# Making the ternary weights of the second feed-forward inside the channel mix of the layer ahead of it

## The chip, the cores and the metric

One core of a Trainium2 chip runs the whole program. The metric is the device time in microseconds (us) of one execution, median of several. Of the engines, TensorE (PE in the profile, its weight loads PEld), VectorE (DVE), ScalarE (ACT) and GpSimd (POOL) compute; SyncE (SP) issues most DMAs.

## The reference, cut to what matters

Two layers are computed for x of shape (16, 512, 16, 12): batch, nodes, channels, times. In each layer a conv part (attention over channels, attention over times, an attention over nodes combined with a graph convolution, a temporal convolution, a layer norm) is followed by a feed-forward: in layer 0 a mixture of eight experts, in layer 1 a two-matrix network whose weights are ternary. The change concerns the preparation of those ternary weights:

```python
def _weight_quant(w):
    s = jnp.clip(jnp.mean(jnp.abs(w)), EPS, None)
    w_dq = jnp.clip(jnp.round(w / s), -1.0, 1.0) * s
    return w + jax.lax.stop_gradient(w_dq - w)

# w_up is 1024 x 512, w_down 512 x 1024; EPS = 1e-05
h = _bitlinear(hidden_states, w_up, bits)      # activations rounded to 8 bits, weights ternary
h = jnp.square(jax.nn.relu(h))
out = _bitlinear(h, w_down, bits)
```

Each matrix needs one scalar, the mean of its absolute values, before any of its elements can be rounded.

## The kernel before, in words

The program is a row of stages. Each stage is one block: every engine has its own instruction list in it, the engines talk over semaphores, and all of them meet at the end of a block before the next begins. The stages of the second layer, in order, are `combine` (makes the layer's input from the experts' results), `conv_weights`, `small_attention` "c1" (16 x 16 attention over channels for all 16 items at once), `mix_channels` "m1" (applies it), `small_attention` "t1" (over times), `graph_conv` "g1", `quantise_weights` and `feed_forward`.

`mix_channels` (L524) goes over the 16 items of the batch. For each, SyncE loads the item's normalised rows (384 KB, four buffers), VectorE builds a 96 x 192 x 2 block matrix from the attention (L550, two buffers `k0`, `k1`; it waits until TensorE is done with item b-2), TensorE multiplies (L567, eight products, which the trace records as two each, as all f32 products) and ScalarE copies the sum to the large buffer `shared` (L579). GpSimd has no work in it. The loops are hardware loops of four items a turn.

`graph_conv` is the long stage. Its SyncE list begins with the load of item 0's rows, then calls `prefetch`, which in the second layer is `ternary_loads` (L1655): both raw weight matrices, 2 MB each, go into `shared`, which is free from then on. `quantise_weights` (L1668) comes after it, alone in its block, with 4096 elements to a partition for each matrix: VectorE sums the absolute values (L1684, one instruction for each matrix); TensorE adds up over the partitions by a product with ones (L1700); VectorE makes the scale and its inverse (L1686, L1687) and three passes over each matrix (L1689 multiply and add the rounding constant, L1690 subtract it and take the minimum with 1, L1691 the maximum with -1, written as bf16 to `wup` or `wdn`), then four small instructions (L1692 to L1695). `Chain` (its call is written `step(...)`) makes VectorE wait for the instruction just issued before it goes on.

`small_attention` "c1" has one more duty, in its SyncE list: `clear_retired` sets the semaphores of earlier stages to zero, one instruction each.

Of the kernel before, what the change touches and what calls it, by code (L numbers as in the profile page):

```python
# [16 lines left out]
F32 = mybir.dt.float32  # L17
# [44 lines left out]
def ready(n):  # L62

    return n + 1 + LEAD

def free(n, depth):

    return n + 1 + LEAD - depth

def dma_ready(i):

    return (i + 2) * 16
# [7 lines left out]
class Chain:  # L82

    def __init__(self, eng, sem):
        self.eng, self.sem, self.base, self.k = eng, sem, 0, 0

    def begin(self, base):
        self.base, self.k = base, 0
# [326 lines left out]
                        act.wait_ge(kept[q], dma_ready(B // 2 - 1))  # L416

def small_attention(nc, s, tag, chan, clear=False):

# [11 lines left out]
    with ExitStack() as ctx:  # L432
# [91 lines left out]
def mix_channels(nc, s, tag, xn_rows):  # L524

    with ExitStack() as ctx:
        (xn_in, big_done, mixed, out_done) = s.sems(
            tag,
            "xn_in*4 big_done mixed out_done")
        xnT, big = [s.xnT0, s.xnT1, s.raw0, s.raw1], [s.k0, s.k1]  # L530
        psm = [ctx.enter_context(nc.psum_tensor(f"{tag}_ps{q}", [P, 2, 512], F32)) for q in range(2)]
        with nc.Block() as block:
            @block.sync
            def _(sp):
                for z in range(4):
                    sp.sem_inc(xn_in[z], 16)
                with sp.Fori(0, B // 4) as i:
                    for z in range(4):
                        sp.wait_ge(mixed, free(i * 4 + z, 4))
                        sp.dma_start(xnT[z][0:HALF, :, :], xn_rows[i * 4 + z]).then_inc(xn_in[z], 16)  # L540

            @block.vector
            def _(dve):
                dve.sem_inc(big_done, LEAD)
                with dve.Fori(0, B // 4) as i:
                    for z in range(4):
                        b = i * 4 + z
                        dve.wait_ge(mixed, free(b, 2))
                        for h in range(2):
                            last = nc.vector.tensor_tensor(  # L550
                                big[z % 2][0:HALF, h, :].rearrange("p (c t) -> p c t", t=T),
                                s.rct[0:HALF, bass.ds(b * C, C)].unsqueeze(2).to_broadcast([HALF, C, T]),
                                s.tmask[:, h, 1, :].unsqueeze(1).to_broadcast([HALF, C, T]), ALU.mult)
                        last.then_inc(big_done, 1)

            @block.tensor
            def _(pe):
                pe.sem_inc(mixed, LEAD)
                with pe.Fori(0, B // 4) as i:
                    for z in range(4):  # L560
                        b = i * 4 + z
                        pe.wait_ge(xn_in[z], dma_ready(i))
                        pe.wait_ge(big_done, ready(b))
                        pe.wait_ge(out_done, free(b, 2))
                        for k in range(NK):
                            for h in range(2):
                                last = nc.tensor.matmul(psm[z % 2][:, k // 2, CT * (k % 2):CT * (k % 2) + CT],  # L567
                                                        xnT[z][0:HALF, h, P * k:P * k + P], big[z % 2][0:HALF, h, :],
                                                        start=(h == 0), stop=(h == 1))
                        last.then_inc(mixed, 1)  # L570

            @block.scalar
            def _(act):
                act.sem_inc(out_done, LEAD)
                with act.Fori(0, B // 4) as i:
                    for z in range(4):
                        b = i * 4 + z
                        act.wait_ge(mixed, ready(b))
                        nc.scalar.activation(  # L579
                            s.shared[:, bass.ds(b * (NK * CT), NK * CT)].rearrange("p (a x) -> p a x", a=2),  # L580
                            psm[z % 2][:, :, 0:2 * CT], ACT.Copy).then_inc(out_done, 1)
# [1070 lines left out]
                item_turns(act, turn)  # L1652

def ternary_loads(eng, s, d, loaded):  # L1655

    up, down = raw_ternary(s)
    eng.dma_start(up.rearrange("p (k i) -> p k i", k=NK),
                  d["w_up"].rearrange("(k p) i -> p k i", p=P)).then_inc(loaded, 16)
    eng.dma_start(down.rearrange("p (k n) -> p k n", k=UK),  # L1660
                  d["w_down"].rearrange("(k p) n -> p k n", p=P)).then_inc(loaded, 16)

def raw_ternary(s):
    return s.shared[:, 0:NK * UP], s.shared[:, NK * UP:2 * NK * UP]

def quantise_weights(nc, s, loaded):  # L1668

    W = NK * UP  # L1670
    with ExitStack() as ctx:
        (chain_done, summed) = s.sems("qw", "chain_done summed")
        w = raw_ternary(s)
        t = s.shared[:, 2 * W:3 * W]
        part = ctx.enter_context(nc.sbuf_tensor("qw_part", [P, 2], F32))
        inv = ctx.enter_context(nc.sbuf_tensor("qw_inv", [P, 2], F32))
        ps = ctx.enter_context(nc.psum_tensor("qw_ps", [P, 512], F32))
        with nc.Block() as block:
            @block.vector
            def _(dve):  # L1680
                step = Chain(dve, chain_done)
                for j in range(2):
                    dve.wait_ge(loaded, 32)
                    step(nc.vector.tensor_reduce(part[:, j:j + 1], w[j], AX, ALU.add, apply_absolute_value=True))  # L1684
                dve.wait_ge(summed, 1)
                step(nc.vector.tensor_scalar(s.wscale[:, :], ps[:, 0:2], 1.0 / (P * W), 1e-5, ALU.mult, ALU.max))  # L1686
                step(nc.vector.reciprocal(inv[:, :], s.wscale[:, :]))  # L1687
                for j, dst in enumerate((s.wup, s.wdn)):
                    step(nc.vector.tensor_scalar(t, w[j], inv[:, j:j + 1], MAGIC, ALU.mult, ALU.add))  # L1689
                    step(nc.vector.tensor_scalar(t, t, MAGIC, 1.0, ALU.subtract, ALU.min))  # L1690
                    step(nc.vector.tensor_scalar(dst, t, -1.0, None, ALU.max))  # L1691
                step(nc.vector.tensor_scalar(s.wscale[:, :], s.wscale[:, :], 1.0 / QB, None, ALU.mult))  # L1692
                step(nc.vector.tensor_copy(s.identb[:, :], s.ident[:, :]))
                nc.vector.memset(s.magic[:, :], MAGIC)
                nc.vector.memset(s.minus_magic[:, :], -MAGIC)  # L1695

            @block.tensor
            def _(pe):
                pe.wait_ge(chain_done, 2)
                nc.tensor.matmul(ps[:, 0:2], s.ones[:, :], part[:, :], start=True, stop=True).then_inc(summed, 1)  # L1700

def feed_forward(nc, s, x_in, x_out):
# [496 lines left out]
def build(nc, d, out):  # L2200
# [11 lines left out]
    def sb(ctx, name, shape, dt=F32):  # L2212
        return ctx.enter_context(nc.sbuf_tensor("s_" + name, shape, dt))

    with ExitStack() as top:
# [36 lines left out]
        with ExitStack() as ctx:  # L2252
            s.wscale, s.magic, s.minus_magic = (sb(ctx, n, [P, 2]) for n in ("wscale", "magic", "minus_magic"))
            s.identb = sb(ctx, "identb", [P, P], BF16)
            s.wup, s.wdn = (sb(ctx, n, [P, NK * UP], BF16)[:, :] for n in ("wup", "wdn"))
            with ExitStack() as conv:
                conv_buffers(nc, s, conv, 1)
                (loaded,) = s.sems("loads1", "loaded")
                combine(nc, s, "join", rows(raw_rows), 1e-6, rows(xn_rows), by_partition(x2),
                        prefetch=lambda eng: conv_loads(eng, s, d, 1, loaded))  # L2260
                conv_weights(nc, s, 1, loaded)
                s.sems.retire()
                small_attention(nc, s, "c1", True, clear=True)
                s.sems.reuse()
                (ternary,) = s.sems("loads2", "ternary")
                mix_channels(nc, s, "m1", rows(xn_rows))
# [63 lines left out]
```

## Time and profile before

| | |
|---|---|
| Median of three executions | 1864.14 us (1862.98 to 1868.24) |
| Profiled execution | 1862.88 us |
| Its span, first to last instruction | 1861.1 us |
| PE, DVE, ACT, POOL busy | 77%, 60%, 40%, 34% |
| c1, from its first product | 1189.5 to 1204.0 us |
| m1 | 1204.7 to 1253.4 us |
| t1, from its first product | 1253.7 to 1264.4 us |
| g1 | 1265.4 to about 1578.8 us |
| quantise_weights | 1579.1 to 1603.8 us |
| feed_forward | 1604.4 us to the end |

All times of the trace are counted from the first instruction of the profiled execution. [...] "128x512 f32" is 128 partitions of 512 elements each.

### The profile page before, as it was taken

The numbers are of one execution on the slowest core, as the hardware profiler recorded it, in microseconds if no ns is written. First come the engines' busy times: TensorE is split into PE (matmuls) and PEld (weight loads), VectorE is DVE, ScalarE is ACT, GpSimd is POOL, SyncE is SP. The second block draws the span as 40 slices with busy tenths as digits, with TensorE's granted clock in tenths as the row PEclk, the third lists the DMA queues.
The fourth block names the chain that finished last, engine by engine and source line by source line (L and its number), as shares of the span: only waits on it lengthen the run. The fifth ranks groups of instructions, "written<-read, shape, count | busy, mean of one in ns | idle before, by whom it ended". The sixth has DMA issues, their size and how long they took to land. (4 is left out here: it accounts for less than half of the span.)

```text
span 1861.1 us, 28248 instructions
## 1 busy us (share of the span) xinstructions
PE 1435.1 (77%) x8462; PEld 1179.6 (63%) x8462; DVE 1113.9 (60%) x2381; ACT 751.4 (40%) x1181; POOL 635.8 (34%) x918
## 2 busy tenths in 40 slices
PE   4578899999464289999999945497999994277676
PEld 4467788887343278888888834395888883155554
DVE  4622488888465654444445335313788886688886
ACT  2412455555242033333333224222555552177775
POOL 1100065556310446555555421000455565011111
PEclk7778899999697579999999965697999997588988
DMA  6423012221374046556555377343122121112221
GB/s 200 144 82 88 9 60 76 68 68 60 113 229 150 12 121 124 108 97 130 122 120 110 38 200 221 99 113 124 44 76 68 59 76 51 43 51 83 94 76 60
DMA packets 95966, 179.95 MB, mean 97 GB/s; under 512 B 13937, under 2 KB 31905, under 8 KB 95909
## 3 DMA queue, kind: packets, MB, share of 16 engines
q1 hardware_dynamic: 71828, 135.52, 23.1%
q0 software_dynamic: 16384, 31.51, 9.8%
q10 hardware_dynamic: 7696, 12.22, 2.1%
q8 instruction: 29, 0.48, 0.1%
q14 instruction: 29, 0.23, 0.0%
HBM read 113.12 MB, written 66.10 MB: 96 GB/s over the span
## 5 line engine op out<-in xcount | busy, mean ns | idle before, releaser
L731 PE MATMUL g_y<-L_z,L_pt 128*128 128x192 f32 x1024 | 197.5, 337 | 1.5 <-ACT L_pt L944 0.5
L889 POOL TENSOR_TENSOR L_xr<-L_xr,L_lnb 128x192 f32<-128x192 f32 x128 | 106.3, 859 | 208.1 <-DMA L_xr<-x 112.2
L731 PEld LDWEIGHTS g_y<-L_z,L_pt 128*128 128x128 f32 x1024 | 167.4, 194 | 6.8 <-ACT L_pt L944 6.8
L1269 POOL DMA_INDIRECT sums<-x_yo,x_places x64 | 103.0, 1609 | 136.4 <-ACT x_yo L1472 126.3
L936 ACT ACTIVATE L_e<-g_s,L_nm 128x512 f32<-128x512 f32 x128 | 88.0, 687 | 79.2 <-DVE L_nm L777 78.2
L699 PE MATMUL g_z<-L_kw,L_xnT 96*128 96x192 f32 x512 | 97.0, 344 | 26.1 <-DVE L_v L807 26.1
L699 PEld LDWEIGHTS g_z<-L_kw,L_xnT 96*128 96x128 f32 x512 | 87.1, 198 | 38.2 <-DVE L_v L807 38.2
L1381 DVE TENSOR_TENSOR x_mid<-ex_g,x_sig 128x480 f32<-128x480 f32 (+1 forms) x48 | 31.3, 653 | 132.8 <-ACT x_sig L1463 125.5
L896 POOL TENSOR_TENSOR L_t<-L_rstd 128x48 f32<-128x48 f32 x96 | 29.2, 305 | 224.5 <-DVE L_rstd L831 219.5
L777 DVE TENSOR_REDUCE L_nm<-g_s 128x1 f32<-128x512 f32 x128 | 87.5, 684 | 27.6 <-PE g_s L708 26.8
L786 DVE SCALAR_TENSOR_TENSOR L_p<-L_e,L_rl,L_adj 128x512 f32<-128x512 f32 x128 | 99.2, 775 | 4.7 <-DVE L_rl L784 0.3
L944 ACT ACTIVATE L_pt<-g_t 128x512 f32<-128x512 f32 x128 | 75.9, 593 | 48.1 <-PE g_t L716 47.9
L716 PE MATMUL g_t<-s_ident,L_p 128*128 128x128 f32 x512 | 77.6, 274 | 9.7 <-DVE L_p L786 9.7
L906 POOL TENSOR_TENSOR L_d<-L_d,L_lng 128x192 f32<-128x192 f32 x128 | 72.4, 598 | 35.7 <-DVE L_d L837 35.7
L1811 PE MATMUL ff_u<-s_wup,ff_q1s 128*96 128x512 bf16 x256 | 79.7, 468 | 5.4 <-DVE ff_q1s L1896 4.0
L716 PEld LDWEIGHTS g_t<-s_ident,L_p 128*128 128x128 f32 x512 | 63.2, 141 | 30.6 <-DVE L_p L786 25.5
L1254 POOL DMA_INDIRECT x_xin<-xn_rows,x_index x64 | 64.8, 1012 | 51.2 <-DVE x_index L1351 18.6
L1441 ACT ACTIVATE x_xh<-ex_t 128x480 fp32r<-128x480 f32 x64 | 36.5, 570 | 109.3 <-PE ex_t L1297 92.2
L727 PEld LDWEIGHTS g_y<-L_res,L_xnT 97*128 97x128 f32 x512 | 76.4, 196 | 6.4 <-ACT L_y L950 1.1
L1311 PE MATMUL ex_g<-x_xh,x_guh 128*128 128x480 f32 (+1 forms) x192 | 76.6, 399 | 3.1 <-issue 3.1
L1325 PE MATMUL ex_d<-x_wdh,x_hh 128*120 128x512 f32 (+1 forms) x192 | 77.5, 404 | 0.0
L1981 POOL TENSOR_TENSOR ff_yo<-ff_ya,ff_xr 128x768 f32<-128x768 f32 x16 | 29.6, 1852 | 139.0 <-DVE ff_ya L1935 139.0
(281 smaller groups left out, 3843.8 us busy)
## 6 DMA issues: line engine op xcount, KB each, us to landing
xn_rows<-L_xnT SPq DMA_DIRECT2D x48, 384.0 KB, 3.5
L_xnT<-xn_rows SPq DMA_DIRECT2D x48, 384.0 KB, 3.4
x<-L_y SPq DMA_DIRECT2D x32, 384.0 KB, 2.5
L_xa<-in_x SPq DMA_DIRECT2D x16, 384.0 KB, 3.9
L_raw<-xn_rows SPq DMA_DIRECT2D x16, 384.0 KB, 3.4
L_xr<-in_x SPq DMA_DIRECT2D x16, 384.0 KB, 3.4
L_xa<-x SPq DMA_DIRECT2D x16, 384.0 KB, 3.9
sums<-L_raw ACTq DMA_DIRECT2D x16, 384.0 KB, 3.1
```

The costliest lines, as they stand in the source:

```text
L699: last = nc.tensor.matmul(psz[:, k // 2, CT * (k % 2):CT * (k % 2) + CT], xnT[q][0:HALF, h, P * k:P * k + P], kw[q][0:HALF, h, NPROJ:], st ...
L716: last = nc.tensor.transpose(pst[k % 2][:, P * c:P * c + P], pr[k % 2][:, P * c:P * c + P], s.ident[:, :])
L727: nc.tensor.matmul(out[:, HALF * h:HALF * h + HALF], xnT[q][0:HALF + 1, h, P * k:P * k + P], s.res[0:HALF + 1, h, :], start=(h == 0), stop ...
L731: last = nc.tensor.matmul(out, pt[k % 2][:, P * c:P * c + P], z[q][:, c, :], start=False, stop=(c == NK - 1))
L777: nc.vector.tensor_reduce(s.nm2[:, k % 2:k % 2 + 1], pss[k % 2][:, :], AX, ALU.max, negate=True).then_inc(nmax_done, 1)
L786: nc.vector.scalar_tensor_tensor(out=pr[k % 2][:, :], in0=e[k % 2][:, :], scalar=s.rl[:, k % 2:k % 2 + 1], in1=s.adj[:, k, :], op0=ALU.mul ...
L889: last = nc.gpsimd.tensor_tensor(v_, v_, gain(s.lnb), ALU.add)
L936: nc.scalar.activation(e[k % 2][:, :], pss[k % 2][:, :], ACT.Exp, bias=s.nm2[:, k % 2:k % 2 + 1], accum_out=s.l[:, k % 2:k % 2 + 1]).then_ ...
L1269: nc.gpsimd.indirect_dma_start(sums, row(places[e % 2][:, 1, t:t + 1]), yo[t % 4][:, :], None, compute_op=ALU.add).then_inc(sent[t % 4], 16)
L1311: last = nc.tensor.matmul(ps_[z][0:size, 0:SN], w[:, k, off + at:off + at + size], x[q][:, k, SN * c:SN * c + SN], start=(k == 0 and x is ...
L1325: last = nc.tensor.matmul(psd[t % 2][0:ST, :], h[0:size, j, ST * t:ST * t + ST], w[0:size, j, :], start=(j == 0 and h is hh and w is wdh), ...
L1811: last = nc.tensor.matmul(psu[0:HALF, c, :], q1s[q][:, k, HALF * h:HALF * h + HALF], wup[:, k, 512 * c:512 * c + 512], start=(k == 0), sto ...
```

## The change

`quantise_weights`, `ternary_loads` and the prefetch in g1 go. A class `Ternary` takes their place; it cuts each matrix into eight chunks of 128 x 512, which lie in sixteen buffers of the conv part that c1, m1 and the stage between don't use. Its sixteen loads of 256 KB stand at the head of SyncE's list in c1. Its arithmetic stands in VectorE's list of m1, between the block matrices of the items, and the product over the partitions stands in TensorE's list of m1 after item 7. VectorE's loop, and TensorE's, of `mix_channels` are written out or split for it, in both layers.

```diff
@@ small_attention, SyncE
+                if ternary:
+                    ternary.loads(sp)
                 if clear:
                     s.sems.clear_retired(sp)
@@ mix_channels, VectorE
-                with dve.Fori(0, B // 4) as i:
-                    for z in range(4):
-                        b = i * 4 + z
-                        dve.wait_ge(mixed, free(b, 2))
...
+                def big_matrix(b):
+                    if b >= 2:
+                        dve.wait_ge(mixed, ready(b - 2))
...
+                if ternary:
+                    big_matrix(0)
+                    big_matrix(1)
+                    ternary.begin(dve)
+                    for b in range(2, HB):
+                        big_matrix(b)
+                        for c in range(3 * b - 6, min(3 * b - 3, 16)):
+                            last = ternary.magnitude(c)
+                    ternary.step(last)
+                    big_matrix(HB)
+                    big_matrix(HB + 1)
+                    ternary.scales(dve, psq)
+                    for b in range(HB + 2, B):
+                        big_matrix(b)
+                        ternary.round(range(2 * (b - HB - 2), 2 * (b - HB - 2) + 2))
+                    for c in range(12, 16, 2):
+                        ternary.round(range(c, c + 2))
+                else:
+                    for b in range(B):
+                        big_matrix(b)
@@ mix_channels, TensorE
+                with pe.Fori(0, B // 8) as i:
+                    for z in range(4):
+                        mix(i * 4 + z, z, i)
+                if ternary:
+                    ternary.across(pe, psq)
+                with pe.Fori(B // 8, B // 4) as i:
+                    for z in range(4):
+                        mix(i * 4 + z, z, i)
@@ in place of ternary_loads and quantise_weights
+class Ternary:
+    CHUNK = 512
+    CHUNKS = NK * UP // CHUNK
...
+    def loads(self, eng):
+        up, down = self.d["w_up"].rearrange("(k p) i -> k p i", p=P), self.d["w_down"].rearrange("(k p) n -> k p n", p=P)
+        for c in range(self.CHUNKS):
+            at = self.CHUNK * (c % 2)
+            eng.dma_start(self.raw[c], up[c // 2][:, at:at + self.CHUNK]).then_inc(self.loaded, 16)
+        for c in range(self.CHUNKS):
+            eng.dma_start(self.raw[self.CHUNKS + c], down[c]).then_inc(self.loaded, 16)
+
+    def begin(self, dve):
+        self.step = Chain(dve, self.chain_done)
+        dve.wait_ge(self.loaded, 32 * self.CHUNKS)
+
+    def magnitude(self, c):
+        return self.nc.vector.tensor_reduce(self.part[:, c:c + 1], self.raw[c], AX, ALU.add, apply_absolute_value=True)
+
+    def across(self, pe, ps):
+        pe.wait_ge(self.chain_done, 1)
+        self.nc.tensor.matmul(ps[:, 0:2 * self.CHUNKS], self.s.ones[:, :], self.part[:, :], start=True,
+                              stop=True).then_inc(self.summed, 1)
+
+    def scales(self, dve, ps):
+        nc, s, step = self.nc, self.s, self.step
+        dve.wait_ge(self.summed, 1)
...
+        step(nc.vector.reciprocal(self.inv[:, :], s.wscale[:, :]))
...
+    def round(self, cs):
+        nc, s, step = self.nc, self.s, self.step
+        for c in cs:
+            j = c // self.CHUNKS
+            last = nc.vector.tensor_scalar(self.raw[c], self.raw[c], self.inv[:, j:j + 1], MAGIC, ALU.mult, ALU.add)
+        step(last)
+        for c in cs:
+            last = nc.vector.tensor_scalar(self.raw[c], self.raw[c], MAGIC, 1.0, ALU.subtract, ALU.min)
+        step(last)
+        for c in cs:
+            at = self.CHUNK * (c % self.CHUNKS)
+            nc.vector.tensor_scalar((s.wup, s.wdn)[c // self.CHUNKS][:, at:at + self.CHUNK], self.raw[c], -1.0, None, ALU.max)
@@ build
-                graph_conv(nc, s, "g1", rows(xn_rows), by_partition(x2), by_partition(x3),
-                           prefetch=lambda eng: ternary_loads(eng, s, d, ternary))
-                quantise_weights(nc, s, ternary)
+                graph_conv(nc, s, "g1", rows(xn_rows), by_partition(x2), by_partition(x3))
```

`scales` has eight small instructions of at most 128 elements: a sum over the chunks, the two of L1686 and L1687, and the four of L1692 to L1695 of before. B is 16 and HB is 8.

## Rows read from the trace of the kernel before

**Rows 1.** Busy time by stretch: engine busy us (instructions), granted clock, DMA share, GB/s.
```profile
1189.40:1196.30 6.90, 6.71 (x96) 3.71 (x96) 0.00 (x0) 0.00 (x0) 0.00 (x0) 0.79 0.01 2
...
1208.40:1213.50 5.10, 5.04 (x18) 5.05 (x19) 0.00 (x0) 0.00 (x0) 0.00 (x0) 0.57 0.61 168
1213.50:1229.10 15.60, 15.60 (x98) 15.60 (x97) 3.73 (x12) 4.87 (x6) 0.00 (x0) 1.00 0.54 151
...
1253.50:1259.10 5.60, 5.41 (x128) 4.89 (x128) 0.00 (x0) 0.00 (x0) 0.00 (x0) 1.00 0.03 6
1579.00:1604.00 25.00, 0.59 (x2) 0.50 (x2) 23.51 (x14) 0.00 (x0) 0.00 (x0) 0.50 0.00 0
```

**Rows 2.** Timeline, quantise_weights, start of feed_forward: start us, us, engine, line, what, [idle<-releaser].
```profile
1579.11 8.88 DVE L1684 TENSOR_REDUCE qw_part<-L_shared 128x1 f32<-128x4096 f32 x2 [2.84 <-PEq L615]
...
1588.04 0.59 PE L1700 MATMUL qw_ps<-qw_part,s_ones 128*128 128x2 f32 x2 [29.89 <-DVE qw_part L1684]
...
1589.13 2.35 DVE L1689 TENSOR_SCALAR L_shared<-L_shared,qw_inv 128x4096 f32<-128x4096 f32 x1
1591.52 2.29 DVE L1690 TENSOR_SCALAR L_shared<-L_shared 128x4096 f32<-128x4096 f32 x1
1593.84 2.29 DVE L1691 TENSOR_SCALAR s_wup<-L_shared 128x4096 bf16<-128x4096 f32 x1
...
1603.72 0.06 DVE L1695 MEMSET s_minus_magic<- 128x2 f32 x1
1604.39 5.40 SPq L1758 DMA_DIRECT2D ff_xa<-x  x3
```

**Rows 3.** Timeline, second layer's first small_attention and the start of its mix.
```profile
1189.53 6.71 PE L453 MATMUL c_psp<-L_shared,L_wc 128*32 128x256 f32 x96 [5.07 <-PEq L191]
...
1203.73 0.28 DVE L517 COPY L_rct<-c_psf 96x128 f32<-96x128 f32 x1
1204.70 1.16 DVE L550 TENSOR_TENSOR L_k<-L_rct,s_tmask 96x192 f32<-96x192 f32 x4 [0.69 <-PEq L558]
1204.83 0.94 SPq L540 DMA_DIRECT2D L_xnT<-xn_rows  x2
...
1208.46 7.56 PE L567 MATMUL m_ps<-L_k,L_xnT 96*128 96x192 f32 x32 [4.97 <-DMA L_xnT<-xn_rows]
```

**Rows 4.** Timeline, middle and end of that mix, first products of the next attention.
```profile
1213.58 0.62 DVE L550 TENSOR_TENSOR L_k<-L_rct,s_tmask 96x192 f32<-96x192 f32 x2 [7.73 <-PE m_ps L567]
...
1216.18 0.62 DVE L550 TENSOR_TENSOR L_k<-L_rct,s_tmask 96x192 f32<-96x192 f32 x2 [1.97 <-PE m_ps L567]
...
1234.38 0.62 DVE L550 TENSOR_TENSOR L_k<-L_rct,s_tmask 96x192 f32<-96x192 f32 x2 [1.98 <-PE m_ps L567]
...
1252.56 0.81 ACT L579 ACTIVATE L_shared<-m_ps 128x768 f32 x1 [1.79 <-PE m_ps L567]
...
1253.67 5.41 PE L453 MATMUL t_psp<-L_shared,L_wt 128*32 128x192 f32 x128 [1.25 <-PEq L532]
```

**Rows 5.** Timeline, g1: SyncE issues item 1's rows; TensorE first uses them.
```profile
1266.94 4.15 SPq L625 DMA_DIRECT2D L_xnT<-xn_rows  x1
...
1295.70 1.88 PE L691 MATMUL g_z<-L_xnT,L_kw 96*96 96x512 f32 x4
```

**Rows 6.** DMA, 1265 to 1285 us: packets, queue (share of 16 engines), issue (us to landing).
```profile
DMA packets 2272, 5.77 MB, mean 288 GB/s; under 512 B 96, under 2 KB 96, under 8 KB 2272
...
L_shared<-in_w_down SPq DMA_DIRECT2D x1, 2048.0 KB, 14.9
```

**Rows 7.** Timeline, a pair of independent 512-wide passes in feed_forward, and its follower.
```profile
1615.93 0.88 DVE L1888 TENSOR_SCALAR ff_q1f<-ff_tn,ff_sc 96x512 f32<-96x512 f32 x2
1616.73 0.22 DVE L1893 TENSOR_SCALAR ff_dq<-ff_am,s_wscale 96x2 f32<-96x2 f32 x1
```

**Rows 8.** One line's instructions, from 1180 us on: duration ns min/median/max, first and last start.
```profile
L777 DVE TENSOR_REDUCE L_nm<-g_s x64: 675/683/694, 1284.8 to 1551.1; 128x1 f32<-128x512 f32 x64
...
L1913 DVE TENSOR_SCALAR ff_q<-ff_sq x16: 678/1430/2115, 1632.4 to 1844.6; 96x1024 bf16<-96x1024 f32 x16
```

More of the change, by code:

```diff
@@ L531, in mix_channels @@
         psm = [ctx.enter_context(nc.psum_tensor(f"{tag}_ps{q}", [P, 2, 512], F32)) for q in range(2)]
+        psq = ctx.enter_context(nc.psum_tensor(f"{tag}_psq", [P, 512], F32)) if ternary else None
         with nc.Block() as block:
@@ L544, in _ @@
                 dve.sem_inc(big_done, LEAD)
-                with dve.Fori(0, B // 4) as i:
-                    for z in range(4):
-                        b = i * 4 + z
-                        dve.wait_ge(mixed, free(b, 2))
[L549 to L554, printed above, removed]
+                def big_matrix(b):
+                    if b >= 2:
+                        dve.wait_ge(mixed, ready(b - 2))
+                    for h in range(2):
+                        last = nc.vector.tensor_tensor(
+                            big[b % 2][0:HALF, h, :].rearrange("p (c t) -> p c t", t=T),
+                            s.rct[0:HALF, b * C:b * C + C].unsqueeze(2).to_broadcast([HALF, C, T]),
+                            s.tmask[:, h, 1, :].unsqueeze(1).to_broadcast([HALF, C, T]), ALU.mult)
+                    last.then_inc(big_done, 1)
+                if ternary:
[18 more added lines that the diff above has]
+                        big_matrix(b)
             @block.tensor
@@ L558, in _, with mix @@
                 pe.sem_inc(mixed, LEAD)
-                with pe.Fori(0, B // 4) as i:
-                    for z in range(4):
[L561 to L570, printed above, removed]
+                def mix(b, z, i):
+                    pe.wait_ge(xn_in[z], dma_ready(i))
+                    pe.wait_ge(big_done, ready(b))
+                    pe.wait_ge(out_done, free(b, 2))
+                    for k in range(NK):
+                        for h in range(2):
+                            last = nc.tensor.matmul(psm[z % 2][:, k // 2, CT * (k % 2):CT * (k % 2) + CT],
+                                                    xnT[z][0:HALF, h, P * k:P * k + P], big[z % 2][0:HALF, h, :],
+                                                    start=(h == 0), stop=(h == 1))
+                    last.then_inc(mixed, 1)
+                with pe.Fori(0, B // 8) as i:
+                    for z in range(4):
+                        mix(i * 4 + z, z, i)
[4 more added lines that the diff above has]
+                        mix(i * 4 + z, z, i)
             @block.scalar
@@ L1652, in _ @@
                 item_turns(act, turn)
[L1655 to L1700, printed above, removed]
@@ new lines, with __init__ @@
+class Ternary:
+    CHUNK = 512
+    CHUNKS = NK * UP // CHUNK
+    def __init__(self, nc, s, d, loaded):
+        self.nc, self.s, self.d, self.loaded = nc, s, d, loaded
+        (self.chain_done, self.summed) = s.sems("qw", "chain_done summed")
+        wide = (s.e0, s.e1, s.p0, s.p1, s.pt0, s.pt1)
+        slabs = (s.xa0, s.xa1, s.xr0, s.xr1, s.y0, s.y1, s.d0, s.d1, s.sqr, s.na)
+        self.raw = [t[:, :] for t in wide] + [t[:, :, :].rearrange("p k x -> p (k x)")[:, 0:self.CHUNK] for t in slabs]
+        self.part, self.inv = s.part, s.inv
+    def loads(self, eng):
[17 more added lines that the diff above has]
+        dve.wait_ge(self.summed, 1)
+        step(nc.vector.tensor_reduce(s.wscale[:, :], ps[:, 0:2 * self.CHUNKS].rearrange("p (j c) -> p j c", j=2), AX,
+                                     ALU.add))
+        step(nc.vector.tensor_scalar(s.wscale[:, :], s.wscale[:, :], 1.0 / (P * NK * UP), 1e-5, ALU.mult, ALU.max))
+        step(nc.vector.reciprocal(self.inv[:, :], s.wscale[:, :]))
+        nc.vector.tensor_scalar(s.wscale[:, :], s.wscale[:, :], 1.0 / QB, None, ALU.mult)
+        nc.vector.tensor_copy(s.identb[:, :], s.ident[:, :])
+        nc.vector.memset(s.magic[:, :], MAGIC)
+        nc.vector.memset(s.minus_magic[:, :], -MAGIC)
+    def round(self, cs):
[10 more added lines that the diff above has]
+            nc.vector.tensor_scalar((s.wup, s.wdn)[c // self.CHUNKS][:, at:at + self.CHUNK], self.raw[c], -1.0, None, ALU.max)
@@ L2254, in build @@
             s.identb = sb(ctx, "identb", [P, P], BF16)
+            s.part, s.inv = sb(ctx, "part", [P, 16]), sb(ctx, "inv", [P, 2])
             s.wup, s.wdn = (sb(ctx, n, [P, NK * UP], BF16)[:, :] for n in ("wup", "wdn"))
@@ L2262, in build @@
                 s.sems.retire()
-                small_attention(nc, s, "c1", True, clear=True)
+                (quantised,) = s.sems("loads2", "ternary")
+                ternary = Ternary(nc, s, d, quantised)
+                small_attention(nc, s, "c1", True, clear=True, ternary=ternary)
                 s.sems.reuse()
-                (ternary,) = s.sems("loads2", "ternary")
-                mix_channels(nc, s, "m1", rows(xn_rows))
+                mix_channels(nc, s, "m1", rows(xn_rows), ternary)
                 small_attention(nc, s, "t1", False)
-                graph_conv(nc, s, "g1", rows(xn_rows), by_partition(x2), by_partition(x3),
-                           prefetch=lambda eng: ternary_loads(eng, s, d, ternary))
-                quantise_weights(nc, s, ternary)
+                graph_conv(nc, s, "g1", rows(xn_rows), by_partition(x2), by_partition(x3))
             feed_forward(nc, s, by_partition(x3), node_major(out))
```

4 lines of the change are left out of this document (2 added, 2 removed).

## The prediction

> **What bounds the kernel now.** I read the profile in this order. The page's busy shares come first: TensorE 77%, VectorE 60%. These are averages over stages with different limits and say little about one edit. The chain of waits breaks off at the last instructions, so I cut the run into stages by the timeline and asked for the busy time of each. The reader should look for stretches in which one engine works alone. There are two kinds here. In the 25 us of the weight preparation VectorE is busy for 23.51 us, TensorE for 0.59 and nobody else at all [rows 1]: everything there is on the path. In the channel mix m1 it is the other way round: TensorE is busy for 15.60 of 15.60 us at the full clock and VectorE for 3.73 [rows 1]. The timeline shows the beat: VectorE starts item 2's block matrix at 1213.58 and item 3's at 1216.18, so an item takes 2.60 us, of which VectorE works 0.62 and is idle 1.97 until TensorE is done [rows 4]. The change moves the first kind of work into the second kind of hole. The questions are whether it fits, what is left over, and what else hangs on the order of the queues.
>
> **What goes.** The weight preparation starts on VectorE at 1579.11, and SyncE issues the first load of feed_forward at 1604.39 [rows 2]. Without the stage, that load comes where VectorE's first reduction now comes; it has a few semaphore instructions ahead of it. Those cost about 0.04 us each: in m1 SyncE issues its first load at 1204.83 after four, VectorE starts at 1204.70 after one [rows 3]. So feed_forward begins at about 1579.2, 25.2 us earlier. Nothing is late in its place: g1 waits for its own last store before its block ends, with or without the stage. The prefetch in g1 goes as well. SyncE then no longer sits 4.15 us on the issue of item 1's rows [rows 5], but TensorE first uses those rows at 1295.70, 25 us after that issue is through [rows 5], so I take nothing for it; a gain of up to 1 us in g1's start goes to the range.
>
> **The loads, moved to c1.** Two issues of m1 take 0.94 us [rows 3]; sixteen at that pitch take 7.5 us from 1189.5, to 1197.0. Behind them on SyncE stand only the semaphore clears, about 63 by my count of the names, at 0.04 us 2.7 us: SyncE is through by 1199.7, against the last VectorE instruction of c1 at 1203.73 [rows 3]. [...] On the DMA engines little else runs in c1 (2 GB/s) [rows 1]. The last of the old loads landed 14.9 us after its issue, 4.2 MB together with 1.6 MB of other data at a mean of 288 GB/s [rows 6]. At that rate 4.2 MB are 14.6 us, with some 2 us to the first bytes: 1206. The loads of m1 are issued at 1204.83 and TensorE takes them up at 1208.46 [rows 3]; they share the engines with the tail. I take 0.5 us of delay, bounds 0 (all landed by 1204.8) and 2.5 (the tail is served first).
>
> [...]
>
> **The sums of absolute values, items 2 to 7.** The nearest row of 512 elements is the row maximum at 0.683 us [rows 8]; three take 2.05, with the block matrix 2.67 against the 2.60 us of an item, less about 0.06 of overlap for each that does not wait for its forerunner. TensorE wants a block matrix one item after VectorE is released to build it, so VectorE may lag 1.9 us before TensorE stands. Cost 0; if each reduction took 0.9 us, the lag would be 3 us by item 7 and the cost about 1.
>
> **TensorE's product over the partitions** stands after item 7 and waits for the sums, which are ready two items earlier. At the low clock it took 0.59 us [rows 2]; here I take 0.4, between 0.2 and 0.6. Behind it wait items 8 to 15. The small steps of the scales (some 1.2 us with their waits) lie on VectorE behind item 9's matrix and are over before it is released for item 10. The split loops: 0.2 us for both layers, bounds 0 and 1.
>
> **The rounding, items 10 to 15 and after.** This is the part that does not fit. A round takes two chunks through three passes. A pair of 512-element passes with a scalar from memory takes 0.88 us, and the follower starts 0.80 after the pair did [rows 7]. The second and third pass are 0.06 cheaper for each instruction (2.35 against 2.29) [rows 2], so 0.76 for a pair; a chained step adds 0.04 (1589.13 plus 2.35 to 1591.52). One round is 0.88 + 0.04 + 0.76 + 0.04 + 0.76, less 0.06 of overlap: 2.42 us. With the matrix, 3.07 us against the 2.60 of an item: VectorE falls back by 0.47 an item, from a slack of 1.95. TensorE therefore stands only before item 15, for about 0.4. But the work runs on. VectorE is released for item 10 at 1234.38 [rows 4]; six matrices of 0.62, eight rounds of 2.42 and 0.2 for waits are 23.3 us, to 1257.7. The block ends now with ScalarE's copy at 1252.56 + 0.81 = 1253.4 [rows 4]. So 4.3 us of the rounding stick out. Bounds: at the old rate without any cost for the smaller pieces (6.93 us a matrix, 1.73 a round) nothing sticks out; at 0.683 for each of the 48 passes [rows 8] a round is 4.1 and 17.7 us stick out. I keep 4.3 because the pair in rows 7 has the same engine, kind and length.
>
> **TensorE's clock after the longer stand.** [...] Now t1 starts 1.25 us after TensorE's last product, at 1.00, and its 128 records of products take 5.41 [rows 1, 4]. In the new kernel TensorE idles from about 1252.9 to 1258.0, some 5 us. [...] c1 streams as many columns (96 times 256 against 128 times 192) and took 6.71 us at a clock of 0.79 after an idle of 5.07 [rows 1, 3]: 1.3 us more. I take 1.7, between 1.3 and m1's 2.5; the lower bound is 0. g1 starts at the low clock either way.
>
> **The sum.** 1862.88 (profiled execution; span 1861.1) - 25.2 + 4.3 + 1.7 + 0.4 + 0.5 + 0.2 = 1844.8 us. The median shown is 1.3 above the profiled execution; I put half of that on top: 1845.5.
>
> **The rivals.**
> 1. *The tail is cheaper.* The passes overlap better or t1 stays at the full clock. Without the last two terms and with 2.5 us less tail: 1844.8 - 1.7 - 2.5 = 1840.6. For it: TensorE's state is not a matter of idle time alone. Against it: three starts after idles near 5 us were all slow.
> 2. *VectorE's passes are dearer in m1.* A line with 1024 elements varied from 0.68 to 2.12 us [rows 8]. At a mean of 0.55 instead of 0.42 for a pass, 48 passes give 6 us more: 1851; at 0.683, 13.4 more: 1858. Against it: the dear cases lie in feed_forward, where GpSimd works; in m1 it has nothing, and the old passes in a quiet stage ran at 0.56 ns an element.
> 3. *The loads are served one after another and hold up the mix: slower than before.* VectorE waits for all sixteen before item 2's matrix, and behind that matrix stand all the others; TensorE needs it at 1216.2. A single load of m1 takes 1208.46 - 1204.83 = 3.6 us to arrive; sixteen in a row, 58 us, last until 1247.5, and item 2 starts 32 us late: 1844.8 + 32 = 1877. It decides the sign from the point at which the loads land 18 us after 1216, below about 95 GB/s. Against it: 288 GB/s for the same bytes [rows 6].
> 4. *No change*, if g1 or feed_forward start later for a reason not seen: I find none.
>
> **Chances.** Forecast, 1842.5 to 1849: 0.70. Rival 1: 0.12. Rival 2: 0.13. Rival 3: 0.03. Rival 4: 0.02. Leaving one in ten out on each side gives 1840.5 to 1852.5. About 0.3% (5.6 us) is what a measurement of this kernel can tell from no change. Faster than 1858.5: 0.95; within: 0.03; slower: 0.02.
>
> **What would show it.** The first load of feed_forward should come at about 1586 (1604.4 less 25.2 and plus the 7 us that c1 to t1 grow by). In m1, items 2 to 14 should keep 2.60 us on TensorE; a first gap before item 2 means late loads, gaps from item 11 on mean dearer passes. VectorE should end m1 some 4 us after ScalarE, and t1's first 128 records of products should take 6.7 to 8 us at a clock near 0.75. If m1 plus t1 grow by more than 9 us or less than 4, the step on the rounding is wrong; if feed_forward, measured from its first load, is longer than the 257 us it has now, something that I don't name was given back there.

## The result and the profile after

The changed kernel takes 1845.76 us in the median of four executions (1842.13 to 1847.77), the kernel before 1864.12 (1862.98 to 1868.24): a ratio of 0.9902, with a 95% interval of 0.9877 to 0.9928. The forecast was 1845.5, the range 1840.5 to 1852.5. A second set of executions gave 1846.48 against 1862.88, 0.9908 (0.9893 to 0.9924). The profiled execution has a span of 1844.0 us, 17.1 less than before.

The first fence is the timeline of the changed kernel from c1 to t1 (columns as in [rows 2]). It is the counterpart of [rows 3, 4] and shows the three new passes of the rounding, lines 1737, 1740 and 1744.

```profile
1188.93 6.71 PE L455 MATMUL c_psp<-L_shared,L_wc 128*32 128x256 f32 x96 [5.08 <-PEq L191]
...
1202.98 0.28 DVE L519 COPY L_rct<-c_psf 96x128 f32<-96x128 f32 x1
1203.65 1.16 DVE L553 TENSOR_TENSOR L_k<-L_rct,s_tmask 96x192 f32<-96x192 f32 x4 [0.39 <-PEq L443]
1204.47 0.95 SPq L543 DMA_DIRECT2D L_xnT<-xn_rows  x2
...
1208.28 7.35 PE L590 MATMUL m_ps<-L_k,L_xnT 96*128 96x192 f32 x32 [5.54 <-DMA L_xnT<-xn_rows]
1213.15 0.62 DVE L553 TENSOR_TENSOR L_k<-L_rct,s_tmask 96x192 f32<-96x192 f32 x2 [8.34 <-PE m_ps L590]
...
1215.67 0.62 DVE L553 TENSOR_TENSOR L_k<-L_rct,s_tmask 96x192 f32<-96x192 f32 x2
...
1231.07 0.29 PE L1718 MATMUL m_psq<-s_part,s_ones 128*128 128x16 f32 x2
...
1234.10 0.62 DVE L553 TENSOR_TENSOR L_k<-L_rct,s_tmask 96x192 f32<-96x192 f32 x2 [1.36 <-PE m_ps L590]
...
1234.64 0.87 DVE L1737 TENSOR_SCALAR L_e<-L_e,s_inv 128x512 f32<-128x512 f32 x2
1235.55 0.76 DVE L1740 TENSOR_SCALAR L_e<-L_e 128x512 f32<-128x512 f32 x2
...
1236.35 0.76 DVE L1744 TENSOR_SCALAR s_wup<-L_e 128x512 bf16<-128x512 f32 x2
...
1237.03 0.61 DVE L553 TENSOR_TENSOR L_k<-L_rct,s_tmask 96x192 f32<-96x192 f32 x2
...
1252.40 0.81 ACT L611 ACTIVATE L_shared<-m_ps 128x768 f32 x1 [1.79 <-PE m_ps L590]
...
1256.05 0.42 DVE L1744 TENSOR_SCALAR s_wdn<-L_na 128x512 bf16<-128x512 f32 x1
...
1256.77 6.94 PE L455 MATMUL t_psp<-L_shared,L_wt 128*32 128x192 f32 x128 [4.51 <-PEq L535]
```

Three readings. SyncE issues m1's first load at 1204.47, 1.21 us after the end of c1's last VectorE instruction (1202.98 + 0.28), where it used to be 0.82 [rows 3]. VectorE starts item 10's matrix at 1234.10 and item 11's at 1237.03, that is 2.93 us for a matrix and a round of two chunks. TensorE's items stay at 2.60 us all the same, since VectorE had time in hand. And the last chunk ends at 1256.47, 3.3 us after ScalarE's last copy (1252.40 + 0.81), so that t1's first products begin after 4.51 us of idle and take 6.94 us.

```profile
1213.20:1228.80 15.60, 15.60 (x98) 15.60 (x98) 13.26 (x29) 4.86 (x7) 0.00 (x0) 1.00 0.53 151
1228.80:1253.20 24.40, 23.46 (x145) 23.16 (x144) 20.59 (x63) 8.08 (x10) 0.00 (x0) 1.00 0.34 97
1253.20:1256.70 3.50, 0.00 (x0) 0.00 (x0) 3.17 (x9) 0.01 (x1) 0.00 (x0) 0.97 0.00 0
1256.70:1263.70 7.00, 6.93 (x128) 5.04 (x128) 0.00 (x0) 0.00 (x0) 0.00 (x0) 0.77 0.02 5
```

The loads, by the DMA view of 1189 to 1209 us (columns as in [rows 6]): the last chunk was issued at 1197.35 and landed 6.5 us later, at 1203.9, ahead of m1's own loads.

```profile
DMA packets 2789, 5.14 MB, mean 257 GB/s; under 512 B 288, under 2 KB 288, under 8 KB 2787
...
L_e<-in_w_up SPq DMA_DIRECT2D x2, 256.0 KB, 3.1
...
L_na<-in_w_down SPq DMA_DIRECT2D x1, 256.0 KB, 6.5
```

The stage between g1 and feed_forward is gone; the timeline goes straight from g1's last VectorE work to the first load of feed_forward. That work ends at 1580.38 (1579.42 + 0.96) and the load is issued at 1583.54, a gap of 3.16 us; in the kernel before, with the stage, it was 28.12.

```profile
1579.42 0.96 DVE L876 TENSOR_TENSOR L_y<-L_d,L_xr 128x768 f32<-128x768 f32 x1 [2.34 <-POOL L_d L938]
1583.54 5.67 SPq L1802 DMA_DIRECT2D ff_xa<-x  x3
```

### The profile page after: what moved, and what is told of

Read it like the earlier page. It is cut to its first block and busy times, and to the rows that moved or that the text cites. A ratio compares the mean times of both kernels' runs of the same rounds, so it can differ in the third digit from the quotient of the medians.

```text
span 1844.0 us, 28228 instructions
## 1 busy us (share of the span) xinstructions
PE 1435.7 (78%) x8462; PEld 1179.5 (64%) x8462; DVE 1119.4 (61%) x2438; ACT 751.4 (41%) x1181; POOL 636.5 (35%) x918
## 3 DMA queue, kind: packets, MB, share of 16 engines
q1 hardware_dynamic: 72564, 135.52, 23.5%
```

## The experiments

The table gives what was read from the timelines of all profiles: t1's first products; the length of g1 (from its first VectorE instruction to the end of its last); the gap from there to feed_forward's first load; the length of feed_forward from that load to the end of the span; and the sum of the last three. Each line is one profiled execution.

```
profile            t1 products     g1     gap  feed_fwd   sum from g1's start
before                    5.41  310.8   28.12     256.7   595.7
before, second            5.41  311.1   28.11     256.9   596.1
before, third             5.41  311.1   28.11     256.7   595.9
changed                   6.94  309.8    3.16     260.5   573.4
changed, second           7.09  311.7    3.17     258.7   573.5
tail_in_t1                5.41  311.5    3.16     258.5   573.1
warm_clock                7.09  311.5    3.16     258.5   573.2
warm_clock_long           5.41  310.8    3.17     257.8   571.8
loads_in_m1               7.08  311.6    3.15     258.4   573.2
loads_split               7.09  311.5    3.16     258.6   573.3
gap_before_ff             7.08  311.6   26.95     258.5   597.0
shift_1us                 7.09  311.6    4.40     257.3   573.3
shift_2us                 7.09  311.6    5.46     260.0   577.1
tail_and_split            5.41  310.9    3.16     258.0   572.1
```

**after_again, before_again, before_third: the same two kernels, profiled again.**

> The changed kernel once more, for a second profile. In the first one feed_forward, measured from its first load, took 260.5 us against 256.7 in the kernel before, and g1 1.0 us less. Theory A (chance: TensorE's low-clock stretches fall otherwise in each execution): here feed_forward may be anywhere from 256 to 261. Theory B (given back by the change, such as by other buffer addresses): again 260 to 261.

> The kernel before once more, for a second profile. Theory A (chance): its feed_forward differs by one to four us from the 256.7 of the first profile. Theory B: 256.7 within 0.5.

The changed kernel: 1846.48 us, feed_forward 258.7 us and g1 311.7. The kernel before: feed_forward 256.9, in a single execution of 1865.93 us. So feed_forward repeated in the kernel before and not in the changed one, where neither 260 to 261 nor 256.7 came. The parts of the changed kernel moved by 1.8 us between its two profiles, but against each other: the sum from g1's start is 573.4 and 573.5. Against 595.7 and 596.1 it is 22.4 us less, where the gap alone fell by 25.0: some 2.5 us were given back behind the change, in both pairs of profiles, which makes chance an unlikely cause. A third profile of the kernel before, a single execution of 1862.75 us:

> A third profile of the kernel before. Theory A (a fixed place in the rhythm): feed_forward 256.5 to 257.0 us again. Theory B (chance): a value nearer 258.5 is as likely.

It gave 256.7 us, as the theory of a fixed place had it (the place of feed_forward's start among TensorE's clock changes, taken up below); the sum is 595.9.

**tail_in_t1: the last two rounds moved from the end of m1 to the head of VectorE's list in t1.**

```diff
@@ mix_channels, VectorE
-                    for c in range(12, 16, 2):
-                        ternary.round(range(c, c + 2))
@@ small_attention "t1", VectorE
+                if tail:
+                    tail.again(dve)
+                    for c in range(12, 16, 2):
+                        tail.round(range(c, c + 2))
                 dve.wait_ge(chosen, 2)
```

> The rounds of the last four chunks (12 to 15) stand at the head of VectorE's list in t1, where it has nothing to do until the first products are through, instead of at the end of m1. Theory A (the rounding that sticks out of m1 costs its length, and through the idle of TensorE the start of t1 at the low clock): m1 ends with ScalarE's copy, 3.3 us earlier, t1's first 128 records take 5.4 us instead of 6.9 and its later small steps about 0.5 less; in all 5 us less than the changed kernel, about 1840.5. Theory B (the stages behind only take up the time in another place, since their TensorE clock falls in its own rhythm): 0 to 2 us less.

Measured: 1840.72 us (1838.74 to 1840.93), ratio 0.9876 (0.9861 to 0.9891) to the kernel before, 5.8 us below the changed kernel on the same chip. Its timeline at the seam:

```profile
1252.56 0.81 ACT L613 ACTIVATE L_shared<-m_ps 128x768 f32 x1 [1.79 <-PE m_ps L592]
...
1253.68 5.41 PE L455 MATMUL t_psp<-L_shared,L_wt 128*32 128x192 f32 x128 [1.25 <-PEq L539]
1253.68 0.88 DVE L1744 TENSOR_SCALAR L_d<-L_d,s_inv 128x512 f32<-128x512 f32 x2 [1.81 <-PEq L539]
...
1258.12 0.42 DVE L1751 TENSOR_SCALAR s_wdn<-L_na 128x512 bf16<-128x512 f32 x1
...
1260.39 0.34 DVE L502 COPY L_sv<-t_psf 10x192 f32<-10x192 f32 x1 [1.84 <-PE t_psf L461]
```

m1 ends with ScalarE's copy, TensorE begins t1 after 1.25 us at the full clock (5.41), and the moved rounds run beside it and are over at 1258.54, 1.8 us before VectorE has its first work of t1. Theory A holds for the time, for the end of m1 and for t1's first products. The excess over its 5 us is within what two medians differ by. (In this profile m1's item 1 took 1.4 us longer than in the others, outside the edited part.)

One part did not come as expected: the small steps behind the products (from their end to VectorE's last copy of t1) take 5.78 us, as in the changed kernel, and not 5.27 as in the kernel before. Both profiles have the same wait of 1.53 us before the last products of t1; the first line is the kernel before, the second tail_in_t1:

```profile
1262.88 1.08 PE L472 MATMUL t_psf<-L_sp,s_foldt 96*96 96x96 f32 x8 [1.53 <-DVE L_sp L507]
```

```profile
1262.89 1.60 PE L474 MATMUL t_psf<-L_sp,s_foldt 96*96 96x96 f32 x8 [1.53 <-DVE L_sp L513]
```

The granted clock in that wait was 1.00 before and 0.80 here, and 1.00 against 0.50 in the products behind it.

**warm_clock and warm_clock_long: TensorE kept busy to the end of m1.**

```diff
@@ mix_channels, TensorE, after the last item (12 in place of 6 in warm_clock_long)
+                    pe.wait_ge(ternary.chain_done, 3)
+                    for r in range(6):
+                        nc.tensor.matmul(psq[:, 0:CT], xnT[0][0:HALF, 0, 0:P], xnT[1][0:HALF, 0, 0:CT],
+                                         start=True, stop=True)
```

> Six products of 128x192 with no use follow TensorE's last one in m1, about 3.9 us of work while VectorE rounds the last chunks. Theory A: TensorE's clock stays at its upper level, t1's first 128 records take 5.4 us instead of 6.9; the end of m1 does not move; c1-to-g1 is 1.5 to 2 us shorter than in the changed kernel. Theory B (the slow start of t1 is not the clock but the fetch of its instructions or the data): still 6.9 us.

The six products took 2.11 us instead of 3.9 and left TensorE idle for 2.56 us; t1 began at the low clock all the same, and the run, 1846.95 us, was no faster:

```profile
1251.23 2.11 PE L606 MATMUL m_psq<-L_xnT 96*128 96x192 f32 x12
1255.91 7.09 PE L455 MATMUL t_psp<-L_shared,L_wt 128*32 128x192 f32 x128 [2.56 <-PEq L535]
```

By itself the 7.09 us would have fitted theory B. The longer run decides:

> The six products with no use took only 2.1 us, TensorE still idled for 2.6 us, and t1 began at the low clock. Now twelve of them, some 4.2 us, to within a few tenths of VectorE's end. Theory A (idle of TensorE lowers its clock): it idles about 1.3 us as in the kernel before, t1's first 128 records take 5.4 us instead of 7.1, the stretch from c1's first product to g1 is 1.5 to 2.2 us shorter than in the changed kernel. Theory B (not the clock): 7 us.

```profile
1251.30 4.06 PE L606 MATMUL m_psq<-L_xnT 96*128 96x192 f32 x24
1255.97 5.41 PE L455 MATMUL t_psp<-L_shared,L_wt 128*32 128x192 f32 x128 [0.60 <-PEq L535]
```

With 0.60 us of idle t1's products take 5.41 us, and the small steps behind them 5.27 instead of 5.78: 2.2 us for the clock. The granted clock (columns as in [rows 1]) says the same, first warm_clock, then warm_clock_long:

```profile
1255.90:1263.00 7.10, 7.09 (x128) 6.12 (x128) 0.00 (x0) 0.00 (x0) 0.00 (x0) 0.76 0.01 2
```

```profile
1255.90:1261.40 5.50, 5.41 (x128) 4.88 (x128) 0.00 (x0) 0.00 (x0) 0.00 (x0) 1.00 0.01 3
```

So the slow start of t1 is TensorE's clock. The median, 1843.77 us (ratio 0.9901, 0.9885 to 0.9917), does not tell it from the changed kernel's 0.9908; the timeline does. At the start of t1 the clock was kept after 1.25 and 0.60 us of idle and lost after 2.56 and more. The length of the idle does not decide by itself: 1.53 us further on in t1 were enough in tail_in_t1 and not in the kernel before. And in the second profile of the changed kernel the clock was still at 1.00 through 4.4 us without a product and fell only when t1's products had begun:

```profile
1253.50:1257.90 4.40, 0.00 (x0) 0.00 (x0) 4.01 (x11) 0.81 (x1) 0.00 (x0) 1.00 0.00 0
1257.90:1258.50 0.60, 0.55 (x12) 0.52 (x16) 0.00 (x0) 0.00 (x0) 0.00 (x0) 0.88 0.00 0
```

**loads_in_m1: the sixteen loads at the head of SyncE's list in m1.**

```diff
@@ small_attention "c1", SyncE
-                if ternary:
-                    ternary.loads(sp)
@@ mix_channels, SyncE
+                if ternary:
+                    ternary.loads(sp)
                 with sp.Fori(0, B // 4) as i:
```

> The sixteen loads stand at the head of SyncE's list in m1 instead of c1, ahead of the items' own loads. Theory A (the loads overlap and need some 14.5 us in all; the mix waits for what is not there): TensorE's first product waits for SyncE's 7.5 us of issuing and for the transfers ahead of its rows, some 12 to 15 us more than now, and VectorE's matrix for item 2 is not held up beyond that; 12 to 15 us slower than the changed kernel, about 1859. The loads are then all there before item 2, so its own wait costs nothing. Theory B (loads are served one after another): they need 50 us and more, 1890 and above.

Measured: 1859.96 us (ratio 0.9977, 0.9967 to 0.9987), 13.5 us over the changed kernel's 1846.48 (12.9 by the two ratios to the kernel before), as theory A had it.

```profile
1204.62 0.84 SPq L1705 DMA_DIRECT2D L_e<-in_w_up  x2
...
1213.35 0.95 SPq L543 DMA_DIRECT2D L_xnT<-xn_rows  x2
...
1222.56 7.61 PE L590 MATMUL m_ps<-L_k,L_xnT 96*128 96x192 f32 x32 [18.96 <-DMA L_xnT<-xn_rows]
1227.68 0.62 DVE L553 TENSOR_TENSOR L_k<-L_rct,s_tmask 96x192 f32<-96x192 f32 x2 [22.01 <-PE m_ps L590]
...
1230.21 0.62 DVE L553 TENSOR_TENSOR L_k<-L_rct,s_tmask 96x192 f32<-96x192 f32 x2
```

SyncE issues the items' rows 8.7 us later than it began, TensorE starts at 1222.56, and no idle follows: VectorE goes from item 2's matrix at 1227.68 to item 3's at 1230.21. The rival that the loads are served one after another is out.

**loads_split: the loads of w_down issued by ScalarE.**

```diff
@@ small_attention "c1"; SyncE keeps the loads of w_up
             def _(act):
+                if ternary:
+                    ternary.loads(act, 1)
                 act.wait_ge(proj_done, 1)
```

> The loads of w_down are issued from ScalarE's list in c1, ahead of its first wait, those of w_up from SyncE's as before. In the changed kernel SyncE issues m1's first load 1.21 us after c1's last VectorE instruction instead of 0.82, although the DMA engines are idle by then. Theory A (SyncE's list of c1 is what makes it late): 0.82 again, m1's first product 0.4 us earlier, in all 0 to 0.5 less than the changed kernel; ScalarE is through with eight issues (3.8 us) before its first input comes at 6.7 us. Theory B (it is the order of the code in m1, not the loads): still 1.21.

```profile
1204.19 0.28 DVE L521 COPY L_rct<-c_psf 96x128 f32<-96x128 f32 x1
...
1205.28 1.00 SPq L545 DMA_DIRECT2D L_xnT<-xn_rows  x2
```

c1's last VectorE instruction ends at 1204.47, SyncE's first load comes at 1205.28: 0.81 us, as theory A had it. So with eight of the sixteen loads taken out of SyncE's list of c1 the 0.4 us at m1's first load are gone, although in the changed kernel SyncE waited 2.0 us at the end of c1 (11.1 before). What in a longer list does so the trace doesn't show. The time, 1846.45 us (ratio 0.9905, 0.9889 to 0.9921), doesn't tell 0.4 us.

**gap_before_ff, shift_1us, shift_2us: useless VectorE work between g1 and feed_forward.**

```diff
+def idle_before_ff(nc, s):
+    (spent,) = s.sems("gap", "spent")
+    t = s.shared[:, 0:NK * UP]             # 1024 or 3072 columns in the two shifts
+    with nc.Block() as block:
+        @block.vector
+        def _(dve):
+            step = Chain(dve, spent)
+            for r in range(10):            # once in the two shifts
+                step(nc.vector.tensor_scalar(t, t, 1.0, 0.0, ALU.mult, ALU.add))
```

> A block with ten chained VectorE passes over 128x4096 elements, with no use, stands between g1 and feed_forward, some 23.5 us, about as long as the stage that the change took out. Theory A (feed_forward's length depends on how long TensorE stood before it): measured from its first load it is 256.7 to 256.9 us again, and the run is 21 to 22 us slower than the changed kernel, 1868. Theory B (something else in the changed kernel, or chance): 258.5 or more, and 25 us slower, or any value.

Measured: 1868.62 us (ratio 1.0026, 1.0015 to 1.0037), feed_forward 258.5. The time, 22 us above the changed kernel, is near theory A's figure; but it spans all stages, and two medians differ by a us or two. The profile decides: the sum from g1's start is 23.5 us above the changed kernel's 573.5, of which the gap is 23.8 (26.95 less 3.16), and feed_forward is no shorter. The long idle before feed_forward is not what made it short; theory A falls. But this gap was 26.95 us, and that of the kernel before 28.11. The next two runs took up the 1.2 us between them:

> A block with one useless VectorE pass over 128x1024 between g1 and feed_forward; it moves the start of feed_forward by about 1.15 us. So far feed_forward took 256.7 and 256.9 us where it began 28.1 us after g1's last VectorE work, and 258.5 at 27.0 and at 3.2. Theory A (the length hangs on where the start falls in the rhythm of TensorE's clock changes, which g1 leaves behind in a fixed place; 28.1 and 27.0 differ by 1.1 us): with 1.1 us more than the changed kernel feed_forward takes 256.7 to 257.2 us, and the run is 0.5 us faster to 0 slower than the changed kernel in spite of the added work. Theory B (chance, or something in the changed kernel): 258.5, and 1.1 us slower.

> The same with a pass over 128x3072, a shift of about 2.2 us. Theory A: another length than 258.5 again, with no direction foreseen (a first profile of the changed kernel had 260.5). Theory B: 258.5.

Measured: with the start 1.24 us later feed_forward takes 257.3 us and the run 1844.98 us (ratio 0.9903, 0.9886 to 0.9919), not slower than the changed kernel, with feed_forward 0.1 us above theory A's range; with 2.30 us it takes 260.0, and 1846.76 us (0.9908, 0.9892 to 0.9925). That is another length than 258.5, as theory A had it, which foresaw no direction here. The timelines of the two and of the changed kernel's second profile, in that order, each with the first load of feed_forward and its first output:

```profile
1585.59 5.42 SPq L1814 DMA_DIRECT2D ff_xa<-x  x3
...
1627.82 1.83 POOL L2037 TENSOR_TENSOR ff_yo<-ff_ya,ff_xr 128x768 f32<-128x768 f32 x1 [9.79 <-DVE ff_ya L1991]
```

```profile
1588.69 5.56 SPq L1814 DMA_DIRECT2D ff_xa<-x  x3
...
1630.08 1.83 POOL L2037 TENSOR_TENSOR ff_yo<-ff_ya,ff_xr 128x768 f32<-128x768 f32 x1 [9.47 <-DVE ff_ya L1991]
```

```profile
1586.74 5.38 SPq L1802 DMA_DIRECT2D ff_xa<-x  x3
...
1629.89 1.82 POOL L2025 TENSOR_TENSOR ff_yo<-ff_ya,ff_xr 128x768 f32<-128x768 f32 x1 [10.24 <-DVE ff_ya L1979]
```

From load to first output are 42.2, 41.4 and 43.2 us: in both shifts the later start shortened it, and TensorE came up to its upper clock at an earlier point of the stage. The granted clock of the first 20 us shows it, 0.51 in the changed kernel's second profile, 0.54 in shift_1us and 0.57 in shift_2us; between 18 and 20 us behind the load it was 0.56, 0.89 and 1.00. The first two as stretches (columns as in [rows 1]):

```profile
1586.74:1606.74 20.00, 7.88 (x32) 5.12 (x32) 7.60 (x24) 2.92 (x4) 1.39 (x2) 0.51 0.30 98
```

```profile
1585.59:1605.59 20.00, 7.37 (x32) 5.04 (x32) 7.59 (x24) 3.41 (x4) 1.39 (x2) 0.54 0.29 98
```

The same reading answers for the 1.2 us between the gap of gap_before_ff and that of the kernel before, here in this order, at 0.51 and 0.55; their first outputs came 43.2 and 41.9 us after the load:

```profile
1608.32:1628.32 20.00, 7.86 (x32) 5.12 (x32) 7.59 (x24) 2.75 (x4) 1.39 (x2) 0.51 0.30 98
```

```profile
1604.39:1624.39 20.00, 7.14 (x32) 4.97 (x32) 7.60 (x24) 3.65 (x4) 1.39 (x2) 0.55 0.30 99
```

The other part of the difference comes later. Most outputs follow each other after 14.2 to 14.3 us, one in four or five after 15.0 to 15.4, and the last two after 11.0 and 11.5. With the shift of 2.30 us, as in the first profile of the changed kernel, these last two take 14.1 and 11.0 instead. In the profiles the end of the program so moved by 0 us for a shift of 1.24 and by 3.8 for one of 2.30 (sums 573.3 and 577.1). The profiled execution of shift_2us was the slowest of its four, 1850.82 us against 1845.29 to 1847.74: by the medians the second shift costs 1.8 us over the first, not 3.8.

**tail_and_split: both improvements together.**

> The last four chunks rounded in t1 (5.8 us faster than the changed kernel in its run) and the loads of w_down issued by ScalarE (m1's first load 0.4 us earlier). If the two add up: 0 to 0.5 us below the version with the rounds in t1 alone, 1840.3. If the start of t1 or of m1 is set by the clock's rhythm and not by the list: the same, 1840.7.

Measured: 1839.46 us (1838.15 to 1843.81), ratio 0.9877 (0.9858 to 0.9897). Against 0.9876 for the rounds in t1 alone there is no difference; the 0.4 us at m1's start are in the profile (0.81 again), not in the time. Both have lower medians than the changed kernel by 6 to 7 us; the interval of tail_in_t1 lies wholly below the changed kernel's second one (0.9893 to 0.9924), that of tail_and_split just touches it.

## Why the prediction was right

The time and the mechanisms of the large terms (what goes, the rounding that sticks out, the clock in t1) were right. The sum had one term too few (2.5 us given back) and its terms for c1 to t1, 7.1 us together, were 1.4 us too large: from c1's first product to g1 the changed kernel is 5.75 and 5.65 us longer in the two pairs of profiles whose c1 products take alike (6.71 us, and 8.17 and 8.18). That made up for half of it. That the forecast fell 0.3 us from the first median is luck: the second set's change is 2 us smaller.

- **What goes.** 25.2 forecast; 28.11 less 3.16 is 24.95.
- **The loads.** 0.5 forecast, as a share of DMA bandwidth. The transfers were through at 1203.9, not 1206, and cost nothing. (The forecast's 2 us to the first bytes are near what the trace of the kernel before shows for its small loads, 1.8 to 2.8 us from issue to landing for 0.2 to 144 KB.) SyncE's first load in m1 was 0.4 us late in their stead, but from the start of c1's products to the end of m1's first item (its copy) the changed kernel is only 0.2 and 0.0 us longer in the same two pairs. A small size was right, the reason wrong.
- **The sums of absolute values** cost TensorE nothing: its items 2 to 7 stay at 2.60 us.
- **The product over the partitions and the split loops:** 0.4 and 0.2 forecast. Items 1 to 15 with it take 39.23 us, without it 39.01: 0.22 for both in m1.
- **The rounding.** 4.3 us sticking out forecast; 3.3 measured. A round with its matrix takes 2.93 us, not 3.07: the pairs were sized well (0.87, 0.76, 0.76), but the matrix overlaps with its neighbours and adds 0.53, not 0.62: it starts 0.08 us before the pass ahead of it ends (1236.35 + 0.76 against 1237.03 in the first fence). TensorE never waited for it, where 0.4 us were foreseen before item 15 (no term of the sum, since VectorE ends later).
- **The clock in t1.** 1.7 forecast; 1.5 to 1.7 on the first products and 0.5 on the small steps behind them, 2.2 in all, shown by warm_clock_long. The upper bound of the 1.7, "m1's 2.5", is the 5.10 us of m1's first item at a clock of 0.57 [rows 1] less the 2.60 of the later ones. The slow starts that rival 1 is weighed against are those of c1 and m1 in the kernel before: after 4.97 to 5.08 us of idle the granted clock was 0.50 in the first us of products, in both layers.
- **The missing term.** The prediction took g1 and feed_forward as fixed blocks that only start earlier, and saw no way for a loss there. They lengthened by about 2.5 us in sum; the prediction's own last sign, feed_forward above 257 us, stood for just this. gap_before_ff and the two shifts show that feed_forward's length changes with the moment of its start (257.3 to 260.0 us), and its granted clock with it (0.51 to 0.57 in the first 20 us); with t1's first products kept at the full clock the sum from g1's start is 571.8 and 572.1 in two profiles of three, 573.1 in the third (tail_in_t1, where the small steps of t1 still took 5.78 us), against 573.2 to 573.5 in the others (without gap_before_ff and shift_2us). g1 itself is longer by 0.5 us or so, and its first 31 us show a lower clock there: 0.50 or 0.51 in the eight profiles with 311.5 to 311.7 us, tail_in_t1 among them, and 0.58 or 0.59 in the five with 310.8 to 311.1. Here before, the changed kernel's second profile and warm_clock_long (columns as in [rows 1]):

```profile
1265.44:1296.44 31.00, 22.49 (x62) 15.61 (x63) 9.59 (x20) 6.59 (x13) 2.23 (x4) 0.58 0.56 186
```

```profile
1271.91:1302.91 31.00, 22.75 (x60) 16.39 (x61) 9.04 (x19) 5.98 (x12) 2.23 (x4) 0.50 0.17 51
```

```profile
1267.74:1298.74 31.00, 22.53 (x62) 15.60 (x63) 9.69 (x20) 6.59 (x13) 2.23 (x4) 0.59 0.18 51
```

The first profile of the changed kernel, with 0.57, had the shortest g1 (309.8) and the longest feed_forward (260.5). No run sets g1's clock by itself, so this is a reading of the traces and not a test.

With the measured terms, -24.95 + 3.3 + 2.2 + 0.2 + 2.5 is -16.8; the second set had 1846.48 less 1862.88, that is -16.4, and the first -18.4 with an interval of some 5 us to either side. The 2.5 was read from the same profiles, so this is a balance and not a second proof. Of the rivals, the cheaper tail was true for 1.0 of its 2.5 us and wrong on t1, which did lose its clock; dearer passes and serial loads were not true.

## What to carry to other kernels

The stage of one engine alone was worth nearly its whole length here, once it was spread over another stage's idle slots: 22.2 of its 24.95 us in tail_in_t1 (1862.88 less 1840.72). What is left over belongs where that engine next waits, in the next stage if need be (5.8 us here), since all engines pay for it at the end of a block (3.3 us here), and TensorE here a second time through its clock (2.2 us). In a program whose stages swing between two clocks, as here between 0.50 and 1.00, a few us saved or added ahead of a stage may return changed (here by 1 to 4 us in single profiles), so compare sums over stages from several profiles before looking for a cause in one.

## What was not expected of the hardware

At the start of t1 TensorE lost its upper clock after 2.56 us of idle and kept it after 1.25 and 0.60, and elsewhere in t1 the same 1.53 us went either way. And feed_forward took 256.7, 257.3, 258.5 and 260.0 us with the same instructions, with starts shifted by one or two us. Three profiles of the kernel before agree within 0.2 us, and six profiles with a g1 of 311.5 to 311.7 us and no shift within 0.3 (258.4 to 258.7), so in these the place among the clock changes seems handed on from stage to stage. The changed kernel's first profile (260.5) shows that the same kernel can also take another place.
